# Projections of pairs 4 to 15 from fp32 to three fp32r products, in a kernel of two chained blocks

## The chip, the cores and the metric

The kernel runs on one core of one Trainium2 chip. The metric is the device time of one execution in microseconds, as the median of several runs. Engines are named as in the profile: PE is TensorE (PEld its weight loads), DVE VectorE, ACT ScalarE, POOL GpSimd, SP SyncE.

## The reference

The input is x of shape (32, 512, 256). Two blocks follow each other, each with a residual and a layer norm. The first is a recurrent one over time:

```python
k, v, r = (einsum('btc,oc->bto', mix_of(x, shifted_x), W) for W in (Wk, Wv, Wr))
wkv_out = wkv_scan(spatial_decay / T, spatial_first / T, k, v)
x = layernorm(x + einsum('btc,oc->bto', sigmoid(r) * wkv_out, Wo))
```

The second picks 63 of 512 tokens of each sequence by a router and sends only these through a transformer layer with 16 heads of 16:

```python
weights = (x @ router_w)[..., 0] + router_b[0]
topv, topi = top_k(weights, 64)
x_sel = x[bidx, sorted(topi[:, :63])]
hn = rmsnorm(x_sel, ln1)              # x_sel * rsqrt(mean(x_sel^2) + 1e-6) * ln1
q, kk, v = rope(heads(hn @ wq)), rope(heads(hn @ wk)), heads(hn @ wv)
a = softmax(q kk^T / 4 + m_sel)
x1 = x_sel + (a @ v) @ wo
x2 = x1 + gelu(rmsnorm(x1, ln2) @ w1) @ w2
```

The rows of x2, times the router's weight, take the place of the picked rows; all others stay, and a layer norm ends it. The products that the change touches are `hn @ wq`, `hn @ wk` and `hn @ wv`.

## The kernel before

Each engine has its own instruction stream, written out by hand, and the streams are tied by semaphores; the order in a stream is the order in the code. An engine that waits holds all that stands behind it in its stream.

**First part (to about 480 us).** One period for each of 32 sequences, `period` in each engine's stream. TensorE computes K, V and R (`projections`, L776): per product one fp32 matmul over the first 128 channels (L788) and three fp32r ones over the other half (L793), then the output of the sequence before (`outputs`, L806 and L808). ScalarE has in each period: exp of K twice (L1170, L1172), a reciprocal (L1191), three scaled differences (L1199) and the rounded half (L1200) for the next sequence, later the copy of the output (L1207) and the normed rows of an earlier sequence (`rows_of`, L1229, four operations), which is the last thing ahead of the next L1170. GpSimd adds the mixes (L578) and the low half (L579), which the next K projection waits for. VectorE runs the scans and, from sequence 22 on, the selection of tokens.

**Second part (to about 690 us).** Two sequences make a pair: 2 x 64 slots are the 128 rows of a tile. Pair n has a period, `att_period(n)`, in each engine's stream, in which also other pairs are worked on. TensorE: turn the mask of pair n+1 (`mask_turn`, L896), project q and k of pair n (`project_qk`, L922), turn the probabilities of n-2 (`p_turn`, L937), project v (`project_v`, L930), turn the output of n-3 (`o_turn`), scores of n-1 (`scores`, L976), turn the normed rows hn of n+1 (`hn_turn`, L960), pick the mask (`mask_pick`, L908), values of n-2 (`values`, L994), turn the second norm's rows of n-4 (`hn2_turn`, L1011), turn q and k (`qk_turn`, L984), output projection of n-3 (`project_o`, L1001). In periods 1, 2, 7 and 8 short products (`picks`, L846 and L850) stand in it as well, and in period 6 `slots_turn` (L834).

ScalarE, `att_period(n)` at L1365: the mask's copy (L1363, on VectorE from pair 13 on), the sum of squares for n-4 (`norm2_of`, L1327), the copy of the turned probabilities (`pT_copy`, L1315), which the scores wait for, v's copies (L1287), oT (L1320), hnT of n+1 (`hnT_copy`, L1247: two operations that also multiply by the gain ln1 of each channel), the picked mask (L1342), h2T (L1348), the exponential (L1296), q's and k's copies (L1302, L1307). At the end of periods 10, 11 and 14 a weight of the MLP is rounded (L1336), at the end of 2 and 3 `rows_of` stands.

GpSimd, for q from 0: the second norm of q-4 (L649 to L659), the end of the rotary step (`rope_end`, L641), `normed(q+2)` (L628: row times its norm, from slotval), `x_of(q+2)` (L633, in place), then gathers. `gather_rows` (L613) fetches the picked rows from the output in HBM: pairs 4 to 6 at the end of q=1, 7 to 9 at 3, 10 to 12 at 7, 13 to 15 at 9. The indices for them are made by VectorE (`keep_values`, L1717 to L1727), in `selection_late(n)`, behind `residual(n-3)` (L1806), which waits for `project_o`. VectorE also does the rotary step (L1787, L1789) and the softmax's first half (L1768, L1770, L1772).

The MLP of pairs follows (L1125, L1139), already with fp32r halves, up to 783 us.

Of the kernel before, what the change touches and what calls it, by code (L numbers as in the profile page):

```python
# [7 lines left out]
def rwkv_then_selected_block_kernel(nc, x_chan, w_attn, columns, mask_rows, positions,  # L8
# [42 lines left out]
    PICKED = 272  # L51
    S = 1024
# [10 lines left out]
    with ctx:  # L63
# [106 lines left out]
        w1_hi, w1_lo = (halves[:, at_x + 4 * T + n * 3 * C:at_x + 4 * T + (n + 1) * 3 * C].rearrange("p (m o) -> p m o", o=C) for n in range(2))  # L170
        psK, psV, psR = ps[:, 0:2, :], ps[:, 2:4, :], ps[:, 4:6, :]
# [44 lines left out]
        hn = both(C)  # L216
        hnT = both(CC, P)
# [122 lines left out]
        hnT_done = sem("hnT_done")  # L340
        qk_ready = sem("qk_ready")
# [198 lines left out]
        def _(pool):  # L540
# [82 lines left out]
            def normed(q):  # L623

                pool.wait_ge(rows_in[q % 8], 16 * (q // 8 + 1))
                if q >= 2:
                    pool.wait_ge(hn_turned, q - 1)
                g.tensor_scalar(hn[q % 2], xsel(q), slotval[:, q, 2:3], None, ALU.mult).then_inc(hn_made, 1)  # L628

            def x_of(q):  # L630

                pool.wait_ge(hn_made, q + 1)
                g.tensor_scalar(xsel(q), xsel(q), slotval[:, q, 0:1], None, ALU.mult).then_inc(x_made, 1)  # L633
# [90 lines left out]

            for q in range(NP + 4):
# [17 lines left out]
                if q + 3 < NP:  # L743
                    gather_mask(q + 3)
                if q in (11, 12, 16):
# [22 lines left out]
        def _(pe):  # L768
# [141 lines left out]

            def project_qk(at):
# [9 lines left out]
                for c in range(CC):  # L921
                    last = mm(ps[:, qk_bank(at.n), :], hnT[at.par][:, c, :], wqk[:, c, :], start=(c == 0), stop=(c == CC - 1))  # L922
                last.then_inc(qk_ready, 1)

            def project_v(at):
# [3 lines left out]
                for c in range(CC):  # L929
                    last = mm(ps[:, 4, 0:C], hnT[at.par][:, c, :], wv[:, c, :], start=(c == 0), stop=(c == CC - 1))  # L930
                last.then_inc(v_projected, 1)
# [19 lines left out]
            def hn_turn(at):  # L951
# [3 lines left out]
                if at.had(2):  # L955

                    pe.wait_ge(qT_done, at.n - 1)
                    pe.wait_ge(kblk_done, at.n - 1)
                for c in range(CC):
                    last = nc.tensor.transpose(ps[:, 5, c * P:(c + 1) * P], hn[at.par][:, c * P:(c + 1) * P], ident[:, :])  # L960
# [77 lines left out]
            def att_period(n):  # L1038
# [59 lines left out]
            pe.wait_ge(w2_in, 3 * 16)  # L1098
            pe.wait_ge(clamp_done, B)
# [889 lines left out]
```

## Time and profile before

| | us |
|---|---|
| median of 3 runs | 781.01 (780.63 to 783.65) |
| profiled execution | 784.69 |
| its span, first to last instruction | 783.0 |
| mean granted TensorE clock | 0.965 |

| engine | busy us | share |
|---|---|---|
| PE | 741.6 | 95% |
| DVE | 647.7 | 83% |
| ACT | 516.2 | 66% |
| POOL | 511.7 | 65% |

Busy times of TensorE's matmul records overlap a little; the distance from the start of a group to the start of the next tells more than their length. An fp32 matmul leaves two records, an fp32r one and a transpose leave one. Idle time of an engine stands in brackets behind the instruction that ended it, with what it waited for.

### The profile page before, as it was taken

The page shows a single profiled execution, that of the slowest core. Times are in us where ns is not written, and L with a number is a line of the kernel's source. Part 1 is how long each engine was busy: PE and PEld are TensorE (multiplying, and loading weights), DVE is VectorE, ACT ScalarE, POOL GpSimd, SP SyncE. Part 2 cuts the span into 40 slices and gives each one's busy share as a digit, 9 for nine tenths or more (in the row PEclk, how much of TensorE's full clock was granted, in tenths as well). Part 3 has the DMA queues.
Part 4 walks back from the last instruction along what each step waited for, and adds up shares of the span by engine and source line. Part 5 has one row for each costly group of instructions (what it writes and reads, how often), then busy time and mean ns, then how long its engine had stood idle before and what let it go on. Part 6 is the DMA issues. An engine that isn't in the chain of part 4 may idle for free. (4 is left out here: it accounts for less than half of the span.)

```text
span 783.0 us, 13078 instructions
## 1 busy us (share of the span) xinstructions
PE 741.6 (95%) x4390; PEld 550.7 (70%) x4390; DVE 647.7 (83%) x1324; ACT 516.2 (66%) x983; POOL 511.7 (65%) x495
## 2 busy tenths in 40 slices
PE   7899999999999999999988999999999999999993
PEld 5466666666666666666556576777788777899993
DVE  6698998989989899899999987679956677568784
ACT  2677888888888888878766774757555766632120
POOL 1587887878878788787767667746737683532323
PEclk8999999999999999999999998979989999999998
DMA  8012524233242332422322211224001120000001
GB/s 231 5 40 61 155 68 134 67 106 95 67 134 69 108 94 73 130 68 88 113 68 68 68 47 36 90 81 141 16 14 48 49 82 2 1 2 28 28 15 41
DMA packets 37337, 55.40 MB, mean 71 GB/s; under 512 B 3360, under 2 KB 26528, under 8 KB 37280
## 3 DMA queue, kind: packets, MB, share of 16 engines
q1 hardware_dynamic: 34464, 46.28, 19.6%
q0 software_dynamic: 2816, 8.39, 3.6%
q8 instruction: 32, 0.52, 0.3%
q14 instruction: 25, 0.20, 0.1%
HBM read 35.78 MB, written 18.87 MB: 70 GB/s over the span
## 5 line engine op out<-in xcount | busy, mean ns | idle before, releaser
L793 PE MATMUL ps<-halves 128*128 128x512 f32 x558 | 239.1, 537 | 0.0
L788 PE MATMUL ps<-arena,wa 128*128 128x512 f32 x384 | 206.3, 620 | 15.6 <-DVE arena L1576 6.8
L793 PEld LDWEIGHTS ps<-halves 128*128 128x128 f32 x558 | 107.7, 193 | 100.6 <-issue 92.1
L808 PE MATMUL ps<-wa,arena 128*128 128x256 f32 x512 | 131.7, 380 | 0.0
L594 POOL TENSOR_TENSOR arena<-arena 128x1024 f32<-128x1024 f32 x32 | 76.2, 2382 | 79.7 <-issue 56.3
L578 POOL TENSOR_TENSOR arena<-arena 128x512 f32<-128x512 f32 x93 | 116.5, 1285 | 6.4 <-ACT halves L1200 6.4
L788 PEld LDWEIGHTS ps<-arena,wa 128*128 128x128 f32 x384 | 71.4, 194 | 45.3 <-POOL halves L579 14.2
L1544 DVE TENSOR_TENSOR_SCAN arena<-ewb,ps 128x511 f32<-128x511 f32 x64 | 74.5, 1206 | 30.6 <-ACT ps L1172 29.7
L808 PEld LDWEIGHTS ps<-wa,arena 128*128 128x128 f32 x512 | 87.3, 190 | 6.6
L585 POOL TENSOR_TENSOR arena<-arena 128x1024 f32<-128x1024 f32 x32 | 76.3, 2383 | 22.5 <-ACT arena L1186 22.5
L1571 DVE TENSOR_TENSOR_SCAN arena<-ewb,ps 128x511 f32<-128x511 f32 x64 | 74.1, 1200 | 0.0
L1229 ACT ACTIVATE arena<-arena 128x256 f32<-128x256 f32 x128 | 66.1, 590 | 0.1
L1199 ACT ACTIVATE arena<-arena,cols 128x512 f32<-128x512 f32 x93 | 60.0, 710 | 0.0
L1357 ACT ACTIVATE arena<-ps 128x512 f32<-128x512 f32 x32 | 19.0, 599 | 52.7 <-PE ps L1125 52.7
L1170 ACT ACTIVATE arena<-ps 128x1024 f32<-128x1024 f32 x32 | 32.7, 1021 | 31.4 <-PE ps L793 25.8
L806 PE MATMUL ps<-ident,arena 128*128 128x128 f32 x256 | 49.0, 273 | 1.6 <-DVE arena L1596 1.4
L1125 PE MATMUL ps<-halves 128*128 128x256 f32 x384 | 48.9, 285 | 0.7 <-DVE ewb L1772 0.7
L1585 DVE BATCH_NORM_STATS2 arena<-arena 128x6 f32<-128x256 f32 x128 | 44.8, 412 | 5.4 <-ACT arena L1207 5.2
L572 POOL TENSOR_TENSOR arena<-arena 128x512 f32<-128x512 f32 x31 | 40.3, 1298 | 12.7 <-DMA arena<-x_chan 12.7
L1125 PEld LDWEIGHTS ps<-halves 128*128 128x128 f32 x384 | 47.0, 192 | 1.3 <-DVE ewb L1772 1.1
L1558 DVE SCALAR_TENSOR_TENSOR arena<-ps,euw,arena 128x512 f32<-128x512 f32 x64 | 45.1, 747 | 3.2
L1139 PE MATMUL ps<-halves 128*128 128x256 f32 x384 | 47.2, 283 | 0.0
(231 smaller groups left out, 1522.4 us busy)
## 6 DMA issues: line engine op xcount, KB each, us to landing
arena<-x_chan SPq DMA_DIRECT2D x32, 512.0 KB, 4.3
out<-arena SPq DMA_DIRECT2D x32, 512.0 KB, 3.2
arena<-x_chan SPq DMA_DIRECT2D x64, 127.8 KB, 3.4
wa<-w_attn SPq DMA_DIRECT2D x1, 1024.0 KB, 7.9
wa<-w_up SPq DMA_DIRECT2D x1, 1024.0 KB, 5.7
wa<-w_down SPq DMA_DIRECT2D x1, 1024.0 KB, 5.3
wqk<-w_qk SPq DMA_DIRECT2D x1, 512.0 KB, 5.2
wv<-w_v SPq DMA_DIRECT2D x1, 256.0 KB, 5.5
```

Of the source, the lines that this page charges most:

```text
L578: g.tensor_tensor(xm[s.par][:, m, :], xm[s.par][:, m, :], xs[s.k][:, :], ALU.add)
L585: g.tensor_tensor(ld[s.par][:, :, :], ld[s.par][:, :, :], er[s.par][:, :, :], ALU.add).then_inc(sum_done, 1)
L594: g.tensor_tensor(gg[s.par][:, :, :], num[s.par][:, :, :], ld[s.par][:, :, :], ALU.mult).then_inc(g_ready, 1)
L788: mm(bank[:, o, :], wa[:, m, 0, out_part], xm[s.par][:, m, :], start=True, stop=False)
L793: last = mm(bank[:, o, :], w[:, m, out_part], x[s.par], start=False, stop=(t == 2))
L806: mm(psY[:, j, c * P:(c + 1) * P], xc[s.k][:, c, tokens], ident[:, :], is_transpose=True, start=(c == 0), stop=False)
L808: last = mm(psY[:, j, :], gg[s.par][:, c, tokens], wa[:, 3, c, :], start=False, stop=(c == CC - 1))
L1125: last = mm(ps[:, up_bank(g, k), h * GP * P:(h + 1) * GP * P], w[:, c, chunk], x[g.par][:, c, :], start=(c == 0 and t == 0), stop=(c == CC ...
L1199: a.activation(xm[s.par][:, m, :], diff[:, :], ACT.Copy, scale=mix[:, m:m + 1])
L1229: last = a.activation(xt[s.k][:, j, :], xt[s.k][:, j, :], ACT.Identity, scale=stat[s.par][:, j, S2:S2 + 1], bias=nm[s.par][:, j:j + 1])
L1544: last = v.tensor_tensor_scan(bb[:, c, 1:T], ewb[:, c, 0:T - 1], psK[:, c, 0:T - 1], 0.0, ALU.mult, ALU.add)
L1571: v.tensor_tensor_scan(aa[:, c, 1:T], ewb[:, c, 0:T - 1], psV[:, c, 0:T - 1], 0.0, ALU.mult, ALU.add).then_inc(scan_a_done, 1)
```

## The change

From pair 4 on (SPLIT = 4) q, k and v are each the sum of three fp32r products: high rows with high weight, high rows with low weight, low rows with high weight. A high half is the value rounded to fp32r, a low half the rest.

- The gain ln1 is multiplied into wqk and wv once (`gains_folded`, ScalarE, at the end of periods 16 and 17 of the first part), for all pairs; `hnT_copy` no longer scales.
- The halves of the weights: ScalarE rounds (`wqkv_high`, at the end of periods 1 and 2 of the second part), GpSimd subtracts (`wqkv_low`, both at q=2).
- The halves of the rows: ScalarE writes the high one (`hn_high(n+2)`, ahead of `pT_copy` in period n, from period 2 to 13), from the gathered row itself, and waits for the gather; GpSimd subtracts it from the normed row behind `normed`.
- TensorE turns both halves, with four transposes, and ScalarE copies them with two operations.
- In TensorE's period `project_o(n-3)` now stands ahead of `qk_turn(n)`.

```diff
@@ GpSimd
                 g.tensor_scalar(hn[q % 2], xsel(q), slotval[:, q, 2:3], None, ALU.mult).then_inc(hn_made, 1)
+                if q >= SPLIT:
+                    pool.wait_ge(hn_made, q + 1)
+                    pool.wait_ge(hn_high_made, q - SPLIT + 1)
+                    g.tensor_tensor(hn[q % 2], hn[q % 2], hn_top[q % 2], ALU.subtract).then_inc(hn_low_made, 1)
...
+            def wqkv_low(n, lo, hi, w):
+                pool.wait_ge(wqkv_rounded, n)
+                g.tensor_tensor(lo, w[:, :, :], hi.bitcast(fp32), ALU.subtract).then_inc(wqkv_split, 1)
...
+                if q == 2:
+                    wqkv_low(1, wqk_lo, wqk_hi, wqk)
+                    wqkv_low(2, wv_lo, wv_hi, wv)
@@ TensorE
+            def product(into, at, w, w_hi, w_lo):
+                if at.n < SPLIT:
+                    parts = ((hnT[at.par], w),)
+                else:
+                    hi, lo = hn_hi[at.par], hn_lo[at.par]
+                    parts = ((hi, w_hi), (hi, w_lo), (lo, w_hi))
+                for c in range(CC):
+                    for t, (x, m) in enumerate(parts):
+                        last = mm(into, x[:, c, :], m[:, c, :], start=(c == 0 and t == 0), stop=(c == CC - 1 and t == len(parts) - 1))
+                return last
...
+                if at.n >= SPLIT:
+                    pe.wait_ge(hn_low_made, at.n - SPLIT + 1)
+                    for c in range(CC):
+                        nc.tensor.transpose(ps[:, 5, C + c * P:C + (c + 1) * P], hn[at.par][:, c * P:(c + 1) * P], ident[:, :])
+                rows = hn_top[at.par] if at.n >= SPLIT else hn[at.par]
...
-                qk_turn(at, min(n + 2, NP))
                 if 3 <= n:
                     project_o(pair(n - 3))
+                qk_turn(at, min(n + 2, NP))
@@ ScalarE
+                    a.activation(hn_hi[at.par], ps[:, 5, 0:C].rearrange("p (c k) -> p c k", c=CC), ACT.Copy)
+                    a.activation(hn_lo[at.par], ps[:, 5, C:2 * C].rearrange("p (c k) -> p c k", c=CC), ACT.Copy).then_inc(hnT_done, 1)
+            def gains_folded(w):
+                act.wait_ge(w2_in, 3 * 16)
                 for c in range(CC):
-                    last = a.activation(hnT[at.par][:, c, :], ps[:, 5, c * P:(c + 1) * P], ACT.Copy, scale=gains[:, 0, c:c + 1])
-                last.then_inc(hnT_done, 1)
+                    a.activation(w[:, c, :], w[:, c, :], ACT.Copy, scale=gains[:, 0, c:c + 1]).then_inc(wqkv_scaled, 1)
+            def wqkv_high(hi, w):
+                act.wait_ge(r_ready, B)
+                act.wait_ge(wqkv_scaled, 2 * CC)
+                a.activation(hi, w[:, :, :], ACT.Copy).then_inc(wqkv_rounded, 1)
...
+            def hn_high(at):
+                act.wait_ge(rows_in[at.n % 8], 16 * (at.n // 8 + 1))
+                if at.n >= SPLIT + 2:
+                    act.wait_ge(hn_turned, at.n - 1)
+                a.activation(hn_top[at.par].bitcast(f32r), xsel(at.n), ACT.Copy, scale=slotval[:, at.n, 2:3]).then_inc(hn_high_made, 1)
```

TensorE, from the values of period 8 to the scores of period 9, before. In order: values, hn2_turn, qk_turn, project_o, mask_turn, project_qk, p_turn, project_v, o_turn, scores, hn_turn.

```order
L994 MATMUL ps<-arena 64x34 x16
L1011 MATMUL ps<-ident,arena 128x128 x2
L984 MATMUL ps<-ident,arena 128x128 x4
L1001 MATMUL ps<-wo,arena 128x256 x2
L896 MATMUL ps<-ident,arena 128x128 x4
L922 MATMUL ps<-wqk,arena 128x512 x2
L937 MATMUL ps<-ident,arena 128x128 x8
L930 MATMUL ps<-wv,arena 128x256 x2
L948 MATMUL ps<-ident,arena 128x128 x2
L976 MATMUL ps<-arena 64x128 x16
L960 MATMUL ps<-ident,arena 128x128 x2
```

The same place after:

```order
L1036 MATMUL ps<-arena 64x34 x16
L1053 MATMUL ps<-ident,arena 128x128 x2
L1043 MATMUL ps<-wo,arena 128x256 x2
L1026 MATMUL ps<-ident,arena 128x128 x4
L922 MATMUL ps<-ident,arena 128x128 x4
L947 MATMUL ps<-halves 128x512 x6
L974 MATMUL ps<-ident,arena 128x128 x8
L947 MATMUL ps<-halves 128x256 x6
L985 MATMUL ps<-ident,arena 128x128 x2
L1018 MATMUL ps<-arena 64x128 x16
L999 MATMUL ps<-ident,arena 128x128 x2
L1002 MATMUL ps<-ident,arena 128x128 x2
```

Two and two fp32 matmuls have become six and six fp32r ones, hn_turn has two transposes more, and project_o (now L1043) stands ahead of qk_turn (L1026).

ScalarE, from k's copy of one period to v's copies of the next, with the mask's copy, the sum of squares and pT_copy between them, before:

```order
L1307 ACTIVATE arena<-ps,bm 128x2x128 x2
L1363 ACTIVATE arena<-ps 128x512
L1327 ACTIVATE arena,norm_0<-arena 128x256
L1315 ACTIVATE arena<-ps 128x1024
L1287 ACTIVATE arena<-ps 64x8x16 x4
```

The same place after:

```order
L1368 ACTIVATE arena<-ps,bm 128x2x128 x2
L1432 ACTIVATE arena<-ps 128x512
L1388 ACTIVATE arena,norm_0<-arena 128x256
L1418 ACTIVATE arena<-arena,slotval 128x256
L1376 ACTIVATE arena<-ps 128x1024
L1348 ACTIVATE arena<-ps 64x8x16 x4
```

hn_high (L1418), which waits for a gather, has come ahead of pT_copy (now L1376).

ScalarE in the first part, after, at the end of periods 16 (rows_of L1272, then the new L1300, then exp of K, L1213):

```order
L1250 ACTIVATE arena<-ps 128x1024
L1272 ACTIVATE arena<-arena 128x256 x4
L1300 ACTIVATE wqk<-wqk,cols 128x512 x2
L1213 ACTIVATE arena<-ps 128x1024
L1215 ACTIVATE ps<-ps 128x1024
```

Before, the four operations of rows_of were followed by exp of K directly; in period 17 the new row is `wv<-wv,cols 128x256 x2`.

## Rows read from the trace of the kernel before

**Rows 1.** The page, its first part: busy us, share, instructions.

```profile
PE 741.6 (95%) x4390; PEld 550.7 (70%) x4390; DVE 647.7 (83%) x1324; ACT 516.2 (66%) x983; POOL 511.7 (65%) x495
```

**Rows 2.** Windows: stretch, length, busy of PE, PEld, DVE, ACT, POOL; clock, DMA.

```profile
535.00:546.00 11.00, 9.49 (x108) 7.61 (x107) 10.62 (x22) 8.66 (x24) 7.67 (x10) 1.00 0.60 193
608.61:618.39 9.78, 9.55 (x108) 7.69 (x107) 6.01 (x10) 6.86 (x20) 7.35 (x10) 1.00 0.24 70
```

**Rows 3.** Timeline (start, us, engine, line), scores of pair 3 and VectorE's softmax.

```profile
540.23 0.73 PE L976 MATMUL ps<-arena 32*64 32x128 f32 x32 [1.51 <-ACT arena L1315]
541.55 1.23 DVE L1768 TENSOR_TENSOR ps<-ps,arena 128x1024 f32<-128x1024 f32 x1
```

**Rows 4.** Timeline, the scores of period 10 and the copy ahead.

```profile
611.24 1.03 ACT L1315 ACTIVATE arena<-ps 128x1024 f32<-128x1024 f32 x1 [0.89 <-PE ps L937]
612.52 0.73 PE L976 MATMUL ps<-arena 32*64 32x128 f32 x32 [0.23 <-ACT arena L1315]
```

**Rows 5.** Timeline of the first part, around exp of K and L788.

```profile
254.14 2.07 ACT L1229 ACTIVATE arena<-arena 128x256 f32<-128x256 f32 x4
256.60 1.02 ACT L1170 ACTIVATE arena<-ps 128x1024 f32<-128x1024 f32 x1 [0.40 <-PE ps L793]
...
308.92 0.30 PEld L788 LDWEIGHTS ps<-arena,wa 128*128 128x128 f32 x2 [0.41 <-POOL halves L579]
```

**Rows 6.** Chain that ended last: start, us, engine, line, records.

```profile
608.61 1.72 PE ps L922 x4
...
647.29 0.44 PE ps L896 x4
```

**Rows 7.** Timeline of the first part, L793 in threes; the chain, L1139.

```profile
300.22 1.26 PE L793 MATMUL ps<-halves 128*128 128x512 f32 x3
301.31 1.02 PE L788 MATMUL ps<-arena,wa 128*128 128x512 f32 x2
301.77 1.25 PE L793 MATMUL ps<-halves 128*128 128x512 f32 x3
...
747.82 5.78 PE ps L1139 x48
```

**Rows 8.** ScalarE: line L1320 (ns min/median/max), and the timeline of L1199.

```profile
L1320 ACT ACTIVATE arena<-ps x16: 377/384/394, 530.2 to 683.4; 128x256 f32<-128x256 f32 x16
...
301.30 1.94 ACT L1199 ACTIVATE arena<-arena,cols 128x512 f32<-128x512 f32 x3
```

**Rows 9.** Timeline of ScalarE: pT_copy in periods 3 and 11.

```profile
528.11 1.03 ACT L1315 ACTIVATE arena<-ps 128x1024 f32<-128x1024 f32 x1 [0.45 <-PE ps L937]
...
621.02 1.02 ACT L1315 ACTIVATE arena<-ps 128x1024 f32<-128x1024 f32 x1
```

**Rows 10.** Timeline: gathers (L613), first use of rows, pT_copy of period 2.

```profile
494.39 0.95 POOL L613 DMA_INDIRECT kept<-out,row_i  x1 [0.30 <-issue]
497.37 0.93 POOL L628 TENSOR_SCALAR arena<-kept,slotval 128x256 f32<-128x256 f32 x1 [0.62 <-DMA kept<-out,row_i]
...
510.27 1.10 POOL L613 DMA_INDIRECT arena<-out,row_i  x1 [1.77 <-DMA out<-arena]
...
513.20 1.02 ACT L1315 ACTIVATE arena<-ps 128x1024 f32<-128x1024 f32 x1 [2.63 <-PE ps L937]
...
DMA to landing us min/median/max: 2.7/2.8/4.6
```

**Rows 11.** Timeline of period 8: residual, gather for pair 10, pT_copy.

```profile
584.32 0.42 DVE L1806 TENSOR_TENSOR arena<-ps,arena 128x256 f32<-128x256 f32 x1 [2.46 <-PE ps L1001]
...
586.52 1.24 POOL L613 DMA_INDIRECT arena<-out,row_i  x1 [9.01 <-DVE msk_i L1727]
...
587.49 1.02 ACT L1315 ACTIVATE arena<-ps 128x1024 f32<-128x1024 f32 x1 [1.60 <-PE ps L937]
```

**Rows 12.** Groups by line from 470 to 700 us: busy us, mean ns.

```profile
L641 POOL TENSOR_TENSOR arena<-arena 128x256 f32<-128x256 f32 x32 | 23.7, 760 | 11.7 <-DVE arena L1789 10.9 <-PE ps L960 0.7
```

**Rows 13.** Windows as in rows 2; the third figure from the end is the clock.

```profile
510.00:512.00 2.00, 2.00 (x5) 0.85 (x5) 1.93 (x9) 0.57 (x2) 1.43 (x2) 0.50 0.00 0
520.00:526.00 6.00, 6.00 (x39) 4.90 (x39) 3.22 (x14) 2.52 (x7) 0.00 (x0) 0.50 0.14 44
564.00:570.00 6.00, 6.00 (x43) 5.47 (x42) 3.31 (x6) 2.56 (x6) 2.49 (x3) 0.50 0.14 44
582.00:584.00 2.00, 2.00 (x7) 1.61 (x6) 0.00 (x0) 2.00 (x6) 0.00 (x0) 0.50 0.01 4
595.00:598.00 3.00, 3.00 (x14) 2.67 (x14) 0.68 (x2) 1.96 (x5) 2.70 (x3) 0.50 0.00 0
598.00:657.00 59.00, 57.62 (x639) 46.46 (x638) 41.09 (x70) 40.88 (x112) 39.67 (x51) 1.00 0.17 48
```

More of the change, by code:

```diff
@@ L51, in rwkv_then_selected_block_kernel @@
     PICKED = 272
+    SPLIT = 4
     S = 1024
@@ L216, in rwkv_then_selected_block_kernel @@
         hn = both(C)
+        hn_top = both(C)
         hnT = both(CC, P)
@@ L340, in rwkv_then_selected_block_kernel @@
         hnT_done = sem("hnT_done")
+        hn_low_made = sem("hn_low_made")
+        hn_high_made = sem("hn_high_made")
+        wqkv_scaled = sem("wqkv_scaled")
+        wqkv_rounded = sem("wqkv_rounded")
+        wqkv_split = sem("wqkv_split")
         qk_ready = sem("qk_ready")
@@ L920, in project_qk @@
                     pe.wait_ge(y_read, B)
-                for c in range(CC):
-                    last = mm(ps[:, qk_bank(at.n), :], hnT[at.par][:, c, :], wqk[:, c, :], start=(c == 0), stop=(c == CC - 1))
-                last.then_inc(qk_ready, 1)
+                if at.n == SPLIT:
+                    pe.wait_ge(wqkv_split, 2)
+                product(ps[:, qk_bank(at.n), :], at, wqk, wqk_hi, wqk_lo).then_inc(qk_ready, 1)
             def project_v(at):
@@ L928, in project_v @@
                 selection_b_read(at.n)
-                for c in range(CC):
-                    last = mm(ps[:, 4, 0:C], hnT[at.par][:, c, :], wv[:, c, :], start=(c == 0), stop=(c == CC - 1))
-                last.then_inc(v_projected, 1)
+                product(ps[:, 4, 0:C], at, wv, wv_hi, wv_lo).then_inc(v_projected, 1)
             def p_turn(at):
@@ L958, in hn_turn @@
                     pe.wait_ge(kblk_done, at.n - 1)
+                if at.n >= SPLIT:
[3 more added lines that the diff above has]
+                rows = hn_top[at.par] if at.n >= SPLIT else hn[at.par]
                 for c in range(CC):
-                    last = nc.tensor.transpose(ps[:, 5, c * P:(c + 1) * P], hn[at.par][:, c * P:(c + 1) * P], ident[:, :])
+                    last = nc.tensor.transpose(ps[:, 5, c * P:(c + 1) * P], rows[:, c * P:(c + 1) * P], ident[:, :])
                 last.then_inc(hn_turned, 1)
@@ L1274, in period @@
                     rows_of(at.back(3))
+                if isinstance(at.n, int) and at.n in (16, 17):
+                    gains_folded(wqk if at.n == 16 else wv)
                 if isinstance(at.n, int) and at.n == 23:
@@ L1370, in att_period @@
                     norm2_of(pair(n - 4))
+                if SPLIT <= n + 2 < NP:
+                    hn_high(pair(n + 2))
                 if 2 <= n:
@@ L1393, in att_period @@
                     rows_of(At(0, B - 4 + n))
+                if n == 1:
+                    wqkv_high(wqk_hi, wqk)
+                if n == 2:
+                    wqkv_high(wv_hi, wv)
                 if n in (10, 11, 14):
```

10 lines of the change are left out of this document (added).

## The prediction

> **What bounds the kernel now.** I read the page first: TensorE is busy 95% of the span, the others 65 to 83% [rows 1]. An average like that hides stages, so I then took the windows of single periods. The change touches the attention part, from 485 to 690 us, where pair n has a period. There are three kinds. In the steady ones (pairs 7 to 15) TensorE is busy 9.55 of 9.78 us and VectorE only 6.01: TensorE's order sets the pace [rows 2]. From 535 us on, for pairs 4 to 6, it is VectorE that is full (10.62 of 11.00 us), because the selection of the second group of sequences runs there [rows 2]; the scores of pair 3 are there at 540.96 and VectorE takes them up at 541.55 [rows 3]. And in each period TensorE has one short wait of its own: the scores (L976) stand idle 0.23 us for ScalarE's copy of the turned probabilities (L1315) [rows 4]. That copy can't start before the eight transposes L937 are through, so the queue between the projection and the scores is the tight place.
>
> In the part before, periods of 13.9 us follow each other through a loop: K projection, ScalarE (L1170 to L1200), GpSimd's mixes and low half (L578, L579), next K projection. TensorE waits 0.41 us there for L579 in each period, and ScalarE has only 0.40 us of idle time ahead of L1170 [rows 5]. So work added to ScalarE just ahead of L1170 is hidden for 0.4 us and no more.
>
> **TensorE's own balance.** The fp32 projection of q and k is two products, four records, 1.72 us; that of v, with half the columns, 0.86 us [rows 6]. For an fp32r product of 512 columns the price stands in the first part: from one L793 to the next it is 1.55 us, and this holds one fp32 product (0.86) and three fp32r ones, so (1.55 - 0.86) / 3 = 0.23 us each [rows 7]. Six are 1.38: q and k save 0.34 us a pair. For 256 columns, 48 products of L1139 took 5.78 us, 0.12 each [rows 7]; six are 0.72, so v saves 0.14. Four transposes take 0.44 us, so the two more that turn the low half cost 0.22 [rows 6]. In all 12 x (0.34 + 0.14 - 0.22) = 3.1 us of TensorE work go. That is all the change has to win at the granted clock of the steady periods, and it would be 0.4%.
>
> Little of it arrives. v's 0.14 us is lost where it stands: the scores come after the end of L937 plus the copy (1.02 us) and signals, and the v products only fill that time, so idle time grows from 0.23 to 0.37 [rows 4]. What remains is 0.22 - 0.34 = -0.12 us for each period that TensorE sets. In pairs 4 to 6 VectorE sets the pace, and its work is not touched: zero. For pairs 7, 9, 10, 13 and 14 I count -0.12 each, **-0.6**.
>
> **ScalarE's additions.** The two hnT copies with scale become two copies of 256 columns without: equal within 0.1 us, and they are waited for by nobody soon. New is the high half of the rows (hn_high), one 128x256 operation, ahead of L1315 in the queue. It moves the queue by something between 0.31 us (L1320 takes 0.384 with no per-partition operand [rows 8], less an overlap of some 0.07) and 0.52 (four L1229 with two such operands in 2.07 [rows 5]); it has one such operand, so I take the middle, 0.42. The page "ScalarE: Activation LUTs" of the Trainium skill, section "What ACT_TABLE_LOAD costs", gives 186 ns and 0.833 ns an element, and 93 ns more for each pointer operand, an estimated 0.49 us for one with one such operand, 93 ns of which overlap; the rows agree. In a plain period ScalarE is idle 0.89 us there, so it is hidden [rows 4]. Two extra transposes also push h2T's copy and the exponential behind it by up to 0.2 us; 0.15 taken. Where the idle time is missing, the rest comes through:
> - pair 11: a weight rounding stands ahead and L1315 starts with no idle time [rows 9]: 0.42 + 0.15, less overlap, **+0.5**. Pair 12 has such a rounding too, but no mask copy, so half the idle time of a plain period: **+0.1**. Pair 15: no hn_high, only the 0.15, **+0.1**.
> - pair 3: rounding wv (128x512, 0.52 in the queue, a little less than L1199's 0.61 since it has no per-partition operand) and hn_high against 0.45 us idle [rows 8, 9]: **+0.5**.
> - pair 4: S(3) would be 0.4 later, but VectorE takes it up only 0.6 us after it is there [rows 3], so nothing.
> - rounding wqk at the end of pair 1 (about 1.0 us) falls into 2.63 us idle [rows 10]: nothing.
> - folding the gains in: two 128x512 operations in period 16. Three of L1199 take 1.94 us, 0.61 in the queue each [rows 8], so 1.22 less most of the idle 0.40 and signals: +0.75; in period 17 two of 128x256, 0.8 less 0.4. Together **+1.1**, and the loop gives nothing back since each step of it waits for the one before [rows 5].
>
> **The new wait.** hn_high(q) waits for the gathered row of pair q, and it stands two periods ahead of the pair in ScalarE's queue, in front of L1315. Before, only GpSimd waited for gathers, later. From the start of a gather to the first use of its rows it took 2.98 us (494.39 to 497.37) [rows 10]; the line's landings run from 2.7 to 4.6. Two pairs are close:
> - pair 4: gather at 510.27, rows usable at 513.25, hn_high to 513.67; L1315 began at 513.20 [rows 10]: **+0.45**.
> - pair 10: the gather starts at 586.52, since VectorE's values wait for the residual (L1806, 584.32, 2.46 us idle for project_o), while L1315 began at 587.49 [rows 11]. The swap of project_o and qk_turn helps: these transposes run at half clock there, 0.85 us, so the gather starts at 585.65. Rows usable at 588.63, L1315 at 589.05: 1.55 later. The queue behind it (v's copy, oT, hnT) and on TensorE the scores wait along. With the extra turn (0.22) **+1.75**. Without the help of the swap it is 2.4 and 0.22; with the slowest landing 1.6 more; if the rows come as early as 2.7, 0.3 less.
>
> **GpSimd** gets 0.76 us (a 128x256 tensor_tensor like L641 [rows 12]) for each pair, and once four and two times that or less for wqk and wv. These stand in its queue ahead of x_of, the mask gather and the next rope_end. It is idle from 520 to 526 us, where the two weights fall [rows 13], and in steady periods it is busy 7.35 of 9.78 us [rows 2]. The low half is ready in the period ahead of its turn. The new waits (hn_low_made, wqkv_split) therefore end early: 0. Behind it, if that cover were gone, rope_end would hold qk_turn.
>
> **The swap** of project_o and qk_turn costs nothing: the copy of q that follows qk_turn waits for the exponential anyway, and the transposes, 0.86 us later, end at about the time when it is through; that is good to 0.2 us a period.
>
> **Sum.** -0.6 + 0.5 + 0.1 + 0.1 + 0.5 + 1.1 + 0.45 + 1.75 = +3.9 us, less 0.1 for VectorE's short waits for the residual in its full stretch: **+3.8 us**. The profiled execution took 784.69 us (span 783.0), the median of three is 781.01; the terms are differences, so I add them to the median: **784.8 us**, 0.49% above. The measurement of this kernel can tell about 0.5% (3.9 us), so the forecast sits on that edge.
>
> **Rivals.**
> 1. The clock falls more often (slower). In five places the granted clock was 0.50, that is 1.2 GHz: around 510, 520 to 526, 564 to 570, around 582, 595 to 598 us [rows 13], behind the short products of picks and values (L846, L850, L994) or idle time. From 598 to 657 it is 1.00 throughout [rows 13]. The change thins the steady period: fewer passes, two more transposes, longer idle times, and 1.5 us of new idle time just ahead of the picks of pair 8. A stretch like 595 to 598 costs half its length, 1.6 us or so. One or two more around pair 8: +1.6 to 3.4, 786 to 788. If each second steady period got one, 4 x 1.6: 791. It decides if TensorE's work between the wait and the values no longer keeps the clock. The page "TensorE: Matmul & The Clock Gate" of the Trainium skill, section "Part 4: PE-mode transpose", says that transposes don't count as busy; by that the added ones weaken the clock. The trace has the clock fall behind short products and never in steady periods, so it agrees only in part. Chance 0.20.
> 2. The stalls are not there (about the same time). If the gather of pair 10 lands ahead and the first part's loop takes up the folding, what is left is 3.9 - 1.75 - 1.1 = +1.0 us, 782. For it: ScalarE's rows show idle time in most periods. Against it: the gather's own start at 586.5. Chance 0.17.
> 3. It gets faster. The 3.1 us would all have to arrive (777.9), and one of the half-clock stretches go (1.6 to 3.4 us less), giving 775 to 777. For it: where TensorE is at half clock the saved time doubles. Against it: no projection of pairs 4 to 15 stands in a half-clock stretch but for the start of pair 7's. Chance 0.08.
> 4. The rewrite does not do what it says, as when six fp32r products in a row didn't overlap: three L793 take 1.26 us to the end of the last [rows 7], 0.42 each, six 2.5, and 12 x (2.5 - 1.72) = +9.6, 794. Their starts, 0.23 apart, speak against it: 0.03.
>
> **How the numbers follow.** The forecast's case has 0.52, with 783 to 787 as its own range, split evenly by the 0.5% edge (784.9). Same: 0.26 + 0.17 = 0.43. Slower: 0.26 + 0.20 + 0.03 = 0.49. Faster 0.08. Range for 8 in 10: from 781.0 (the stalls gone) to 789.5 (two or three more half-clock stretches).
>
> **What would show it.** Right: six fp32r records of 0.23 us for q and k; VectorE-bound pairs 4 to 6 with the same 9.8 us; an idle time of about 0.37 us ahead of the scores; ScalarE idle in pair 8 for the DMA of the gather, some 1.5 to 3 us, with TensorE idle next to it; periods 16 and 17 of the first part 0.8 and 0.35 longer. Wrong: half clock in steady periods (rival 1), no wait for the gather (rival 2), or steady periods shorter by 0.3 us and more, which would mean that L1315 is not what the scores wait for.

## The result, and the profile of the changed kernel

| | us | ratio to the kernel before (95% interval) |
|---|---|---|
| kernel before, median of 11 runs | 781.56 | |
| changed kernel, median of 11 runs | 788.88 (784.57 to 791.03) | 1.0096 (1.0074 to 1.0118) |
| changed kernel, its profiled execution | 785.9 (span 784.1) | |

The change costs 7.5 us (5.8 to 9.2), 1% of the time: slower by more than the 0.5% that can be told, in the forecast's direction and inside its range, but twice the sum of +3.8. The profiled execution is the second shortest of the eleven (785.9 us), so I use one of another run as well (a0 below, 790.93 us, span 789.2). The two lie on either side of the median of 788.9.

TensorE's first row of the page, beside [rows 1]; it is now busy 93% and not 95% of a span that is longer:

```profile
PE 733.0 (93%) x4462; PEld 553.8 (71%) x4462; DVE 648.6 (83%) x1324; ACT 523.2 (67%) x997; POOL 523.9 (67%) x509
```

Windows from the scores of pair 0 to those of pair 15, for the kernel before, the changed kernel and its second execution, in this order (stretch, length, busy of PE, PEld, DVE, ACT, POOL, then the clock):

```profile
502.50:669.49 166.99, 159.20 (x1638) 129.85 (x1637) 122.98 (x232) 107.53 (x287) 98.03 (x126) 0.93 0.18 54
```

```profile
500.18:670.66 170.48, 154.21 (x1710) 135.57 (x1709) 123.99 (x232) 113.23 (x299) 110.37 (x140) 0.94 0.18 52
```

```profile
502.49:675.69 173.20, 155.67 (x1710) 136.97 (x1709) 124.01 (x232) 113.34 (x299) 110.36 (x140) 0.93 0.18 52
```

This is the whole result in three rows. Against the kernel before, the second execution has 3.5 us less of busy TensorE (159.20 to 155.67) and 9.7 us more of idle TensorE (7.79 to 17.53), which makes +6.2 us, at the same mean clock of 0.93. From pair 15's scores to the end both take 113.5 us. The start of pair 0's scores, where these windows begin, lies between 497.5 and 503.4 us in the fourteen traces of this case, also in kernels whose first part is the same. So whole spans of single executions are not compared here, only these windows. The change did what it was to do for TensorE, and the time came back as waiting.

Where it came back shows in the scores. Each pair has one group of 16 score products (32 records), so the distance between two groups is the length of a period. "Pair n" is the distance from the scores of n-1 to those of n:

| pair | before | changed | changed, 2nd |
|---|---|---|---|
| 1 | 11.98 | 12.37 | 12.35 |
| 2 | 14.91 | 13.54 | 13.55 |
| 3 | 10.84 | 14.53 | 14.59 |
| 4 | 9.78 | 11.27 | 11.11 |
| 5 | 9.78 | 9.67 | 9.68 |
| 6 | 14.95 | 11.35 | 11.35 |
| 7 | 14.03 | 16.69 | 16.95 |
| 8 | 13.97 | 13.86 | 15.43 |
| 9 | 9.78 | 9.68 | 10.65 |
| 10 | 9.78 | 10.34 | 10.34 |
| 11 to 13 | 29.34 | 29.23 | 29.23 |
| 14, 15 | 17.85 | 17.95 | 17.97 |
| sum | 166.99 | 170.48 | 173.20 |

Three places hold it: pairs 3 and 4, pairs 7 and 8, and in the second execution pair 9. Pair 6 gives 3.6 back. The timeline of the changed kernel at those places (start, us, engine, line; idle time before it in brackets); L1018 is the scores, L1376 pT_copy, L1418 hn_high, L1363 q's copy, L1026 qk_turn:

```profile
507.94 1.10 POOL L624 DMA_INDIRECT arena<-out,row_i  x1 [1.76 <-DMA out<-arena]
...
510.88 0.51 ACT L1418 ACTIVATE arena<-arena,slotval 128x256 fp32r<-128x256 f32 x1 [1.69 <-DMA arena<-out,row_i]
...
512.55 0.73 PE L1018 MATMUL ps<-arena 32*64 32x128 f32 x32 [0.85 <-ACT arena L1376]
...
526.09 0.73 PE L1018 MATMUL ps<-arena 32*64 32x128 f32 x32 [2.05 <-ACT arena L1376]
...
532.52 0.60 PE L1026 MATMUL ps<-ident,arena 128*128 128x128 f32 x4
...
535.08 0.38 ACT L1363 ACTIVATE arena<-ps 128x256 f32<-128x256 f32 x1 [3.28 <-remote]
...
540.62 0.78 PE L1018 MATMUL ps<-arena 32*64 32x128 f32 x18 [3.85 <-ACT arena L1376]
...
584.88 1.24 POOL L624 DMA_INDIRECT arena<-out,row_i  x1 [7.65 <-DVE msk_i L1802]
...
587.93 0.51 ACT L1418 ACTIVATE arena<-arena,slotval 128x256 fp32r<-128x256 f32 x1 [2.40 <-DMA arena<-out,row_i]
588.35 1.00 ACT L1376 ACTIVATE arena<-ps 128x1024 f32<-128x1024 f32 x1
...
613.14 0.73 PE L1018 MATMUL ps<-arena 32*64 32x128 f32 x32 [0.39 <-issue]
```

The predicted waits for the gathers are there (510.88 and 587.93), 2.94 and 3.05 us behind their gathers' starts. The idle times in front of the scores are 0.85, 2.05, 3.85, for pairs 1 to 3. In the kernel before they were 0.45, 0.23 and 1.51, the last in [rows 3], the others here; in a plain period it is 0.39 for 0.23 [rows 4].

```profile
514.48 0.73 PE L976 MATMUL ps<-arena 32*64 32x128 f32 x32 [0.45 <-ACT arena L1315]
529.39 0.73 PE L976 MATMUL ps<-arena 32*64 32x128 f32 x32 [0.23 <-ACT arena L1315]
```

### The profile page after: what moved, and what is told of

It is laid out like the page before. It is cut to its first block and busy times, and to the rows that moved or that the text cites. A ratio compares the mean times of both kernels' runs of the same rounds, so it can differ in the third digit from the quotient of the medians.

```text
span 784.1 us, 13287 instructions
## 1 busy us (share of the span) xinstructions
PE 733.0 (93%) x4462; PEld 553.8 (71%) x4462; DVE 648.6 (83%) x1324; ACT 523.2 (67%) x997; POOL 523.9 (67%) x509
## 5 line engine op out<-in xcount | busy, mean ns | idle before, releaser
L1272 ACT ACTIVATE arena<-arena 128x256 f32<-128x256 f32 x128 | 66.2, 590 | 0.1
L1213 ACT ACTIVATE arena<-ps 128x1024 f32<-128x1024 f32 x32 | 32.6, 1020 | 27.6 <-PE ps L819 23.3
L1168 PE MATMUL ps<-halves 128*128 128x256 f32 x384 | 48.9, 285 | 0.7 <-DVE ewb L1847 0.7
L832 PEld LDWEIGHTS ps<-ident,arena 128*128 128x128 f32 x256 | 35.6, 140 | 16.8 <-issue 1.8
```

Of the source, the lines that this page charges most:

```text
L832: mm(psY[:, j, c * P:(c + 1) * P], xc[s.k][:, c, tokens], ident[:, :], is_transpose=True, start=(c == 0), stop=False)
L1168: last = mm(ps[:, up_bank(g, k), h * GP * P:(h + 1) * GP * P], w[:, c, chunk], x[g.par][:, c, :], start=(c == 0 and t == 0), stop=(c == CC ...
L1272: last = a.activation(xt[s.k][:, j, :], xt[s.k][:, j, :], ACT.Identity, scale=stat[s.par][:, j, S2:S2 + 1], bias=nm[s.par][:, j:j + 1])
```

## Experiments

Each ratio is to the kernel before, measured beside it on the same chip. The median of the kernel before itself moved by some 2 us between these groups (779.9 to 782.1), so ratios are compared. 0.001 is 0.78 us.

| run | what | median us | ratio (95% interval) |
|---|---|---|---|
| a0_after_again | the changed kernel | 790.64 | 1.0110 (1.0071 to 1.0150) |
| a1_no_folding | without the gains' folding | 787.82 | 1.0067 (1.0036 to 1.0099) |
| a2_high_late | hn_high late in all periods | 782.44 | 1.0013 (0.9991 to 1.0034) |
| d1_late_pair10 | hn_high late for pair 10 alone | 783.70 | 1.0035 (1.0008 to 1.0062) |
| d2_late_pairs4to6 | hn_high late for pairs 4 to 6 alone | 784.00 | 1.0052 (1.0027 to 1.0078) |
| b4_old_products | fp32 products, all else kept | 789.02 | 1.0096 (1.0065 to 1.0127) |
| a3_swap_undone | swap undone | 796.61 | 1.0192 (1.0152 to 1.0231) |
| b3_swap_alone | swap in the kernel before | 779.46 | 0.9976 (0.9947 to 1.0004) |
| b1_five_idle | five idle semaphores in the kernel before | 781.24 | 1.0007 (0.9985 to 1.0028) |
| c1_late_and_spread | a2, weight work spread | 779.86 | 1.0003 (0.9978 to 1.0028) |
| e1_spread_no_swap | c1, swap undone | 779.88 | 0.9999 (0.9976 to 1.0022) |
| d3_split7 | c1 with SPLIT = 7 | 781.46 | 0.9987 (0.9965 to 1.0009) |

The distances of the scores in some of their profiled executions, one for each kernel. Two executions of the changed kernel differ by 2.7 us in their sum (the table above), so single rows tell more than sums:

| pair | before | a0 | a2 | d1 | d2 | b4 | c1 | b3 | a3 |
|---|---|---|---|---|---|---|---|---|---|
| 1 | 11.98 | 12.35 | 11.97 | 12.43 | 12.00 | 12.26 | 10.71 | 10.29 | 12.31 |
| 2, 3 | 25.75 | 28.14 | 24.11 | 28.07 | 25.90 | 26.74 | 26.49 | 25.47 | 26.72 |
| 4, 5 | 19.56 | 20.79 | 20.93 | 20.91 | 19.86 | 20.00 | 20.94 | 19.57 | 24.56 |
| 6 | 14.95 | 11.35 | 11.34 | 11.32 | 11.32 | 11.34 | 11.34 | 11.53 | 11.97 |
| 7 | 14.03 | 16.95 | 13.86 | 15.45 | 16.39 | 17.34 | 13.86 | 15.57 | 16.85 |
| 8 | 13.97 | 15.43 | 16.38 | 12.27 | 16.81 | 18.97 | 13.85 | 14.05 | 19.82 |
| 9 | 9.78 | 10.65 | 9.68 | 9.80 | 10.62 | 10.00 | 9.68 | 9.78 | 10.64 |
| 10 | 9.78 | 10.34 | 10.34 | 10.35 | 10.35 | 10.34 | 9.95 | 9.78 | 10.35 |
| 11 to 15 | 47.19 | 47.20 | 47.48 | 47.19 | 47.19 | 48.06 | 47.48 | 47.20 | 47.19 |
| sum | 166.99 | 173.20 | 166.09 | 167.79 | 170.44 | 175.05 | 164.30 | 163.24 | 180.41 |

**The changed kernel again (a0).**

> The changed kernel once more, beside the kernel before on the same chip, as the base for the three runs that follow. Its median was 7.3 us above that of the kernel before (788.88 against 781.56), twice the sum of +3.8. Theory A (local terms, one of them mis-sized): ratio again 1.007 to 1.012, and the trace shows the second part some 3 to 7 us longer in the same places: pair 4, pair 10, pair 3. Theory B (clock): the execution has more half-clock time between 497 and 690 us than the kernel before, by 5 us or more, and the excess over +3.8 is found there.

Measured: 1.011. Theory A's three places are there. Theory B falls in the form I gave it: narrow windows find the clock at 0.50 in five stretches between 500 and 690 us in the kernel before and in a0, 23.9 us in all in each; the first execution of the changed kernel has 20.5. Before: 509 to 513, 520 to 526, 564 to 571, 581 to 584, 595 to 598; in a0: 509 to 512, 529 to 532, 543 to 546, 580 to 587, 597 to 604. Two of them:

```profile
580.50:587.00 6.50, 6.50 (x41) 5.87 (x41) 2.49 (x14) 2.63 (x7) 0.00 (x0) 0.50 0.01 1
597.40:604.00 6.60, 6.60 (x41) 5.97 (x40) 2.48 (x13) 2.78 (x7) 1.84 (x2) 0.50 0.15 40
```

They have moved, which explains single rows of the tables (pair 6's -3.6 is the stretch at 564 gone, pair 8's 15.43 the one at 597, 6.8 us long where the kernel before has 3.4), but their sum has not grown.

**Folding left out (a1).** In `period` of ScalarE, together with the two waits for these operations:

```diff
-                if isinstance(at.n, int) and at.n in (16, 17):
-                    gains_folded(wqk if at.n == 16 else wv)
```

> The gains ln1 are not multiplied into wqk and wv (ScalarE's four operations at the end of periods 16 and 17 are left out, nothing takes their place), so q, k and v lack the factor ln1; all else as in the changed kernel. The prediction's term for them is +1.1 us. Theory A: 1.0 to 1.3 us less than the changed kernel. Rival: the loop of the first part absorbs them, 0 to 0.3 us less. Theory B says nothing against either, since the clock of the first part is not touched.

Measured: 1.0067 against 1.0110, and the intervals overlap, so the medians settle neither the size nor, strictly, the sign. The traces do. K's first weight load of four periods following each other, in the changed kernel:

```profile
236.24 0.30 PEld L814 LDWEIGHTS ps<-arena,wa 128*128 128x128 f32 x2 [0.41 <-POOL halves L590]
...
250.17 0.30 PEld L814 LDWEIGHTS ps<-arena,wa 128*128 128x128 f32 x2 [0.41 <-POOL halves L590]
...
253.09 1.32 ACT L1300 ACTIVATE wqk<-wqk,cols 128x512 f32<-128x512 f32 x2
...
264.80 0.30 PEld L814 LDWEIGHTS ps<-arena,wa 128*128 128x128 f32 x2 [0.78 <-POOL halves L590]
...
267.35 0.90 ACT L1300 ACTIVATE wv<-wv,cols 128x256 f32<-128x256 f32 x2
...
278.74 0.30 PEld L814 LDWEIGHTS ps<-arena,wa 128*128 128x128 f32 x2 [0.41 <-POOL halves L590]
```

13.93, 14.63, 13.94 us: wqk's two operations cost 0.70, wv's nothing. Without them (a1) every period is 13.93, and from pair 0's scores to pair 15's a1 takes 173.17 us, a0 173.20. So the folding costs 0.7 us in the first part and nothing behind it.

**hn_high later (a2, d1, d2).** In ScalarE's `att_period`, for all n (a2), for n == 8 alone (d1), for n < 5 alone (d2):

```diff
-                if SPLIT <= n + 2 < NP:
-                    hn_high(pair(n + 2))
                 if 2 <= n:
                     pT_copy(pair(n - 2))
...
                     hnT_copy(pair(n + 1))
                     mask_keep(pair(n + 1))
+                if SPLIT <= n + 2 < NP:
+                    hn_high(pair(n + 2))
```

> hn_high(n+2) moved in ScalarE's period from ahead of pT_copy to behind hnT_copy and mask_keep; nothing else. The wait for the gather of pairs 4 and 10 then no longer stands in front of the scores. Theory A: 2.2 us less for the two waits and some 0.5 us less for pair 11, so -2.7 us against the changed kernel, at about +4.8 against the kernel before. Theory B: the half-clock time that follows the idle TensorE of pairs 3, 4 and 10 goes too: -4 to -7 us. Third possibility: the operation delays the exponential behind it (h2T_copy, exp_p) by as much as it delayed the scores, 0 to -1 us.

Measured: 1.0013, so 0.97% (7.6 us) of the 1.10% is in the place of this one operation of 0.5 us and its wait. It is more than theory A's 2.7 and at the upper end of theory B. In the window below a2 has 4.5 us less of idle TensorE than a0 (13.0 against 17.5) and 2.6 us less of busy TensorE; of half clock it has 17.1 us, a0 23.9. Theory A's 0.5 us for period 11 did not come: pair 10 takes 10.34 us in both.

```profile
500.92:667.01 166.09, 153.08 (x1710) 134.45 (x1709) 124.53 (x232) 114.64 (x299) 110.47 (x140) 0.95 0.18 54
```

> The changed kernel with hn_high behind mask_keep in period 8 alone (pair 10, whose gather is late); in all other periods it stays ahead of pT_copy. Moving it in all periods took 8 us off (790.64 to 782.44). Theory A: pair 10's wait for the gather is worth 1.75 (its term of the sum); the trace should have the scores of pair 7 idle 0.39 us instead of 1.63 to 1.89 and their distance from those of pair 6 down from 16.95 to 15.2 or less, and the total 2 to 3 us below the changed kernel (ratio 1.007 to 1.009 to the kernel before). Theory B: with the wait goes a half-clock stretch at 597 to 604 us as well, 4 to 5 us less (1.005).

Measured: 1.0035, -0.75% (5.9 us). The scores of pair 7 stand idle 0.38 us, no longer 1.89, and pair 8 takes 12.27 us, since no half-clock stretch follows; from 585 to 650 us the clock is 1.00 throughout:

```profile
585.00:650.00 65.00, 61.33 (x747) 54.88 (x746) 44.32 (x75) 46.15 (x124) 52.94 (x69) 1.00 0.19 54
```

Pairs 7 to 9 together: 43.03 in a0, 37.52 in d1. 1.5 of these 5.5 us is the wait, the rest is what came behind it (half clock, and pair 9's 0.85). Against the first execution (40.23) it is 2.7 us. The ratio rules out theory A and fits theory B.

> The changed kernel with hn_high behind mask_keep in periods 2 to 4 alone (pairs 4 to 6). The sum had 0.45 for pair 4's gather and 0.5 for the queue in pair 3's period. Theory A: 1 us less than the changed kernel (1.008 to 1.010). Theory B, from the distances of the scores' starts: pairs 2 to 4 took 2.8 us more than in the kernel before and 4.4 more than with hn_high late everywhere, through a delayed copy of q in period 3; so 3.5 to 4.5 us less (1.005).

Measured: 1.0052, -0.58% (4.5 us), theory B. Pairs 1 to 4: 48.08 us, in a0 51.60, before 47.51. The two effects add up to 1.33 and not to a2's 0.97, a difference that is smaller than the noise of these four ratios. In the traces a2 has a half-clock stretch at 589 to 596 us again, which d1 lacks.

In d2 and a2 also the odd row of period 3 is gone. ScalarE around q's copy in a2; it starts as soon as the exponential ahead of it is through:

```profile
530.82 1.04 ACT L1357 ACTIVATE arena<-ewb 128x1008 f32<-128x1008 f32 x1 [1.56 <-DVE ewb L1847]
530.92 0.60 PE L1026 MATMUL ps<-ident,arena 128*128 128x128 f32 x4
531.89 0.39 ACT L1363 ACTIVATE arena<-ps 128x256 f32<-128x256 f32 x1
```

But a2 has such a row in another place. ScalarE's copy of the turned high half of pair 9 starts 2.3 us after its transposes have ended, just ahead of the half-clock stretch at 589:

```profile
586.76 0.39 ACT L1292 ACTIVATE halves<-ps 128x256 fp32r<-128x256 f32 x1 [2.46 <-remote]
```

**The products alone (b4).** In `product`, one pass in place of three; the low half of the rows is left out of the product:

```diff
-                    parts = ((hi, w_hi), (hi, w_lo), (lo, w_hi))
+                    parts = ((hn_hi[at.par].bitcast(fp32), w),)
```

> The changed kernel with one fp32 product where it has three fp32r ones: the high half of the rows with the whole weight, for q, k and v. All preparations, transposes, copies and waits stay; the low half of the rows is not in the product, so the output lacks it. By the sum, the fp32r products save 0.34 us a pair for q and k where TensorE sets the pace (pairs 7 to 15) and nothing elsewhere, v's saving is lost in a wait: this kernel 2 to 3.5 us above the changed one (792.5 to 794 if that has 790.6). If both savings arrive: +5.8. If even that of q and k is lost in waits: 0 to +1.

Measured: 1.0096 (1.0065 to 1.0127), beside 1.0110 for a0 and 1.0096 in the changed kernel's first eleven runs. So +5.8 is ruled out. The third case fits best, but the lower end of the first (+2 us) lies inside the intervals. Its windows, the whole stretch and one steady period, and the steady period of the changed kernel:

```profile
499.50:674.55 175.05, 164.66 (x1661) 135.82 (x1660) 123.63 (x232) 113.54 (x299) 110.29 (x140) 0.91 0.17 51
606.15:616.15 10.00, 9.77 (x109) 7.92 (x109) 6.02 (x9) 7.32 (x21) 8.58 (x12) 1.00 0.21 61
```

```profile
603.46:613.14 9.68, 9.29 (x113) 8.29 (x113) 6.01 (x9) 7.08 (x19) 8.36 (x11) 1.00 0.16 45
```

The steady periods are as the sum has them, to 0.02 us: 9.78 + 0.22 for the transposes = 10.00, and 0.32 less for q and k = 9.68; v's part becomes idle time ahead of the scores (0.23 us in b4, 0.39 in the changed kernel). Over the whole stretch TensorE is busy 164.66 us and idle 10.4, against 155.67 and 17.5 in a0: of 9.0 us of work less (some of it because this execution has 30.7 us at half clock), 7.1 became idle time. It is tempting to say that TensorE's work had covered ScalarE's lateness, but for most of the 7.1 us this isn't shown: 3.4 of them are ahead of the scores of pairs 2 and 3 (2.06 and 3.90 in a0, 0.87 and 1.65 in b4), those of pair 2 ahead of the first product that this edit touches, and those of pair 3 behind a late copy of q that b4's trace lacks.

**The swap (a3, b3, e1).** In TensorE's `att_period`; a3 and e1 undo it, b3 makes it in the kernel before:

```diff
-                if 3 <= n:
-                    project_o(pair(n - 3))
                 qk_turn(at, min(n + 2, NP))
+                if 3 <= n:
+                    project_o(pair(n - 3))
```

> TensorE's qk_turn(n) ahead of project_o(n-3) again, as in the kernel before; all else as in the changed kernel. The prediction has the swap at 0, with 0.87 us of help for the gather of pair 10. Theory A: 0 to +1 us. Rival: the swap costs in each period where project_o's 0.44 us delay the turn of q and k, and so their copies and the scores of the next period: -1 to -4 us.

Measured: +0.82% (6.4 us) against a0, the opposite sign of the rival and far more than theory A. ScalarE waits 3.88 us for the gather of pair 10, not 2.47 as in a0, and the clock is at half in 544 to 554 and 595 to 612 us; between 500 and 690 us it is so for 37.5 us:

```profile
594.09 0.51 ACT L1418 ACTIVATE arena<-arena,slotval 128x256 fp32r<-128x256 f32 x1 [3.88 <-DMA arena<-out,row_i]
```

```profile
544.00:554.00 10.00, 9.95 (x57) 9.03 (x58) 7.06 (x12) 4.07 (x12) 4.98 (x6) 0.50 0.28 100
595.20:612.00 16.80, 16.24 (x115) 15.33 (x116) 5.31 (x10) 5.47 (x17) 7.40 (x10) 0.50 0.14 40
```

> The kernel before with project_o(n-3) ahead of qk_turn(n), nothing else. Undoing the swap in the changed kernel cost 6.0 us (796.61 against 790.64). If the swap is worth something by itself (VectorE gets project_o's result earlier in the periods where it waits for it): 1 to 4 us less than the kernel before. If it only helps the waits that the change makes (the gather of pair 10): 0 to -0.5 us. If it is paid for by later copies of q and k: +0.5 to +1.

Measured: -0.24% (-4.1 to +0.3 us). That fits the first two cases and speaks against the third. Pairs 1 and 6 are 1.7 and 3.4 us shorter in its trace, pair 7 1.5 longer.

> The run with hn_high late and the weight work spread (779.86, ratio 1.0003), with qk_turn ahead of project_o again as in the kernel before. In the changed kernel undoing the swap cost 6 us, in the kernel before making it brought 0.4 us or nothing that can be told. If the swap matters only because ScalarE's queue then waited for pair 10's gather: 0 to +1 here (ratio 1.000 to 1.002). If it matters by itself, by giving VectorE the result of project_o 0.4 us (0.9 at half clock) earlier in the periods where the residual is waited for: +2 to +4 (1.003 to 1.005).

Measured: 0.9999, against 1.0003 for c1. Without the waits for gathers the order of the two makes no difference that can be told (0.3%). So what the swap is worth in the changed kernel is the repair of a wait that the change itself makes, with the half clock that comes behind it.

**Numbers of semaphores (b1).** Five declarations added to the kernel before.

> The kernel before with five more semaphores that nobody uses, declared where the changed kernel declares its own, so that all later ones get other numbers, as in the changed kernel. In period 3 of the changed kernel ScalarE's copy of q stood idle 3.28 us for something the trace calls remote, 1.9 us after the turn of q and k had ended; the kernel before has no such row. Theory C (the delay comes with the numbers of the semaphores): such rows appear here, and the time rises by 2 us or more. Theory A and B: no difference, ratio 0.998 to 1.002.

Measured: 1.0007, and no such row; the window from pair 0's scores to pair 15's is 167.01 us, before 166.99. Theory C falls, also because b4 and a2 have the changed kernel's numbers and q's copy in period 3 is on time.

**Towards a better kernel (c1, d3).** c1 is a2 with

```diff
-                if isinstance(at.n, int) and at.n in (16, 17):
-                    gains_folded(wqk if at.n == 16 else wv)
+                if isinstance(at.n, int) and at.n in (16, 17, 18):
+                    gains_folded(*{16: (wqk, range(1)), 17: (wv,), 18: (wqk, range(1, 2))}[at.n])
...
                 if n == 1:
                     wqkv_high(wqk_hi, wqk)
-                if n == 2:
                     wqkv_high(wv_hi, wv)
```

and d3 is c1 with `SPLIT = 7`.

> As the run with hn_high behind mask_keep (782.44), and two more moves: both weight roundings of ScalarE at the end of period 1 of the second part (its trace has ScalarE idle there 2.5 us), and the four gain operations in three periods (one of wqk in 16, both of wv in 17, the other of wqk in 18) since the traces have period 16 0.71 us longer with both of wqk and 17 not longer with both of wv. Theory A: 0.7 + 0.4 us less, 781.3. Theory B: where half-clock stretches fall changes with it, so between 779 and 785.

> As the run with hn_high late and the weight work spread (779.86), with SPLIT = 7: pairs 4 to 6, which VectorE paces, keep the fp32 products and their two transposes. TensorE's saving arrives only where TensorE sets the pace, so nothing is given up: if so 0 to -2 us, the latter if the half-clock stretch at 537 to 541 us goes. If the thinner stretch of pairs 4 to 6 was what kept later half-clock stretches away: +1 to +3.

Measured: 1.0003 and 0.9987. Neither can be told from the kernel before, nor from a2. In c1's trace the three periods with folding cost 0.10, 0.16 and 0.01 us, where wqk's two operations together cost 0.70. The idle time ahead of pair 2's scores is 0.40 (1.66 in a2), but TensorE is at half clock there from 516.5 to 520.5 us and was not in a2, so this can't be put down to the rounding of wv; the next scores wait 2.25 us (1.85 in a2). The best that this form gave is the time of the kernel before.

## Why the prediction came out as it did

The direction was right, the likeliest case (783 to 787) was not: 788.9 lies above it and even above rival 1's first step (786 to 788). That it is inside the range is in part luck. From the scores of pair 0 to those of pair 15 the changed kernel in a0 takes 6.2 us more than the kernel before, and this is the rest of errors of both signs: pairs 2 to 4 cost 3.7 us where the sum has 0.5, pairs 7 to 9 cost 5.3 (2.4 in the first execution) where it has 1.75 for the gather, and pair 6 gave back 3.6 for which it has no term. Without pair 6's gift the time would be some 792 us, an estimate from 788.9 + 3.6, outside the range. Step by step:

- **The row prices held.** Six fp32r products 0.32 us cheaper than two fp32 ones (predicted 0.34), two transposes 0.22 (b4's period against that of the kernel before), a steady period -0.10 (predicted -0.12), idle ahead of the scores 0.39 (0.37). hn_high takes 0.525 us in the median of 12; I had priced its place in the queue at 0.42, and the starts of L1418 and L1376 are 0.42 apart (587.93, 588.35):

```profile
L1418 ACT ACTIVATE arena<-arena,slotval x12: 497/525/541, 510.9 to 640.6; 128x256 fp32r<-128x256 f32 x12
```

  The estimate from the page "ScalarE: Activation LUTs" of the Trainium skill, section "What ACT_TABLE_LOAD costs", was 0.49 and is 0.03 us low against the 0.525 of this trace.
- **The terms of the later pairs held in size**: pair 10's scores (period 11) +0.56 (predicted +0.5), pair 11's +0.09 (+0.1), pairs 14 and 15 +0.1 (+0.1), pair 4's gather +0.37 to 0.39 (+0.45, seen at pair 1's scores). That period 11's +0.56 comes from hn_high's place ahead of pT_copy isn't shown: a2 moves it and keeps the +0.56. Folding is +0.7, not +1.1: the second half of that term, period 17, was hidden.
- **"In pairs 4 to 6 VectorE sets the pace" was wrong.** It is busy 10.62 of 11.00 us there [rows 2], but the distance of the scores of pair 5 is 9.78 before, 9.68 in the changed kernel and 10.00 with fp32 products. It follows TensorE's work to 0.02 us. A window of 11 us was the wrong measure; the distance of the scores was to be had. The sign "pairs 4 to 6 with the same 9.8 us" was wrong for the same reason: they took 14.95 us for pair 6 before, and 11.1 to 11.35 for pairs 4 and 6 after.
- **The step that failed is the pricing of ScalarE's delays one by one, at the clock of the old trace and with nothing behind them.** For pair 3's period I had 0.52 + 0.42 against 0.45 idle, +0.5, and for pair 4 nothing. At the old clock that +0.5 is right. In b4 TensorE is at half clock ahead of pair 2's scores (516.5 to 523.5 us) as it was in the kernel before (519.5 to 526.5); those scores stand idle 0.87 us, and pair 2 takes 15.50 us, +0.59. In the changed kernel this stretch is missing in both traces. TensorE is then ready earlier, the same queue of ScalarE makes it wait 2.05 us, and of what the full clock gives only 1.4 us is left (13.54 against 14.91). The loss stands behind the wait, where the sum has nothing: pair 3 takes 14.53 against 10.84, with half clock from 527 to 531 us and q's late copy; pair 4 takes 1.3 to 1.5 more, with half clock again from 541 us, right behind the idle 3.85 us.

```profile
527.26 0.73 PE L1017 MATMUL ps<-arena 32*64 32x128 f32 x32 [0.87 <-ACT arena L1375]
```

- **Pair 10's gather was seen, its price was not.** The wait itself came out as 1.4 to 1.7 us more idle (0.23 before; 1.63 and 1.89 after), inside the 1.75. But pairs 7 to 9 take 43.0 us in a0, 40.2 in the first execution and 37.8 before: +2.4 to +5.3. d1 (37.5) shows that all of it hangs on this wait. Rival 1 had the mechanism (1.5 us of new idle time just ahead of the picks of pair 8, then half clock) with a chance of 0.20, and took it for additional to the sum; the two executions show that its stretch at 597 us is sometimes 3.4 and sometimes 6.8 us long.
- **Rival 1's clock, as a sum, did not come**: half clock is 23.9 us in the kernel before and in a0, 20.5 in the first execution. The page "TensorE: Matmul & The Clock Gate" of the Trainium skill, section "Part 4: PE-mode transpose", says that a transpose doesn't count as busy in the way that other work does. The two more a period did not bring the clock down where nothing waits: in c1 it is 1.00 from 592.5 to 660 us, with all of them there.

```profile
592.50:660.00 67.50, 63.32 (x768) 55.96 (x766) 49.09 (x81) 49.98 (x133) 46.28 (x61) 1.00 0.15 43
```

- **The swap at "nothing" was right in itself** (b3, e1) and its help for pair 10's gather was underrated: 0.87 us predicted, 1.4 us of wait (3.88 against 2.47), and 6.4 us in time with the longer half clock behind it.
- **Rival 3's half-clock stretch did go** (pair 6, -3.6 us, in every variant but b1), also with the swap alone. It went also where the swap is undone (a3, e1). Why is open; the same short products stand there with the same 1.05 us of idle time ahead of them where it comes (before, b1) and where it doesn't (a0, a3, e1). It hides how much the other pairs lost.

What stays open is pair 3. In five traces with hn_high early in periods 2 to 4 and fp32r products (the profiled one, a0, a1, a3, d1) q's copy in period 3 starts 1.5 to 2.1 us after its transposes, with the releaser given as remote; with hn_high late, or with fp32 products, it does not. The trace doesn't name what held it, and the numbers of the semaphores are not it. One thing is common to these rows and to that of a2 at 586.76: GpSimd starts gathers in the 3 us before each of them, the last or the last but one 1.7 to 2.0 us before the copy. No run tests whether that is the cause. Pair 4's excess, on the other hand, goes with the clock: it takes 11.0 to 11.3 us in the traces with a half-clock stretch of 3.4 us just behind the scores of pair 3 (the profiled one, a0, a1, a2, c1, d1, e1), 14.88 in a3 with one of 10.2 us, and 9.78 to 10.18 in those without. The idle time ahead of it doesn't decide: 1.85 us in a2 with the stretch, 2.15 in d3 without.

## What to carry to other kernels

An operation that waits for a transfer doesn't belong in an engine's stream ahead of the copy that the bound engine waits for, however short it is: here 0.5 us in the wrong place cost 1%. Work taken from the busy engine pays only where its next step doesn't wait for another engine: q's and k's 0.32 us a period arrived, v's part became idle time. Idle time measured beside a half-clock stretch can't be spent once the stretch moves. To see who sets the pace, take the distances between one marker per period (here the scores), not busy shares of a window.

## What the runs showed of the hardware

- The clock's half-speed stretches moved with every edit, as small as one operation's place, and changed single periods by 1.6 to 5 us: pair 8 took 12.27, 13.86, 15.43, 16.38 or 18.97 us with nearly the same work. Their sum between 500 and 690 us ran from 13.7 (c1, b3) over 23.9 (before, a0) to 37.5 us (a3); the longest one came behind the longest wait ahead of pair 7's scores (a3: 3.39 us of idle, then 17 us at half clock), but a2 has 6.8 us at half clock at the same place behind an idle time of 0.39 us.
- The same kernel differed by 2.7 us between two executions in which the waits ahead of the scores of pairs 1 to 8 were the same to 0.3 us, through one stretch of 3.4 or 6.8 us and one late copy (pT_copy ahead of pair 9's scores, which stood idle 1.35 us instead of 0.39).
